# A four-layer graph kernel: layer 1 in another order, layer 2's walks in fp16 halves, layer 1's first halves made at the end of layer 0

## The reference

```
L0: H = adj != 0; h = relu(Dn * H @ (Be * H^T @ (x @ W1^T)) + b1); y = conv(layernorm(h), W2, b2)
L1: q, k, v = x @ W_qk, W_v; w = softmax over nodes(sum_m(q k^T / 8 * adj)); out = w * v
L2: T = rows normalised(adj * exp(leaky_relu(s_i + s_j))); H = sum_k (T^k x) @ Wk[k] + bk[k], k = 0, 1, 2; relu(H)
L3: A = rows normalised(exp(leaky(8 tanh((s_i + s_j) / 8))) * adj) * rowsum(adj); out = A @ x @ w
x = layernorm(x + L(x, adj))        after each of the four layers
```

## Time and profile before

| | |
|---|---|
| time, median of 3 runs | 778.45 us (775.82 to 780.42) |
| the profiled execution | 780.04 us |
| its span, first to last instruction | 778.1 us |
| busy: PE, DVE, ACT, POOL | 708.9, 548.5, 524.2, 320.9 us |
| mean granted clock of TensorE | 0.958 of full speed |

### The profile page before, as it was taken

One profiled execution on the slowest core, in us unless ns is written; L12 is line 12 of the kernel. 1 busy time (PEld: TensorE's weight loads), 2 busy tenths in 40 slices (PEclk: granted clock), 3 DMA queues, 4 the chain that ended last, 5 costly groups with the idle time before them and its releaser, 6 DMA issues.

```text
span 778.1 us, 18246 instructions
## 1 busy us (share of the span) xinstructions
PE 708.9 (91%) x5590; PEld 513.2 (66%) x5590; DVE 548.5 (70%) x1648; ACT 524.2 (67%) x1161; POOL 320.9 (41%) x402
## 2 busy tenths in 40 slices
PE   5899999999999983887787799999999997999995
PEld 5677777777777751554454566666666665878884
DVE  4888888888878742688878456666565654577995
ACT  4668887767777763566666555757575666688886
POOL 2243455434344434445454212323131313566773
PEclk9999999999999996999988699999999999899998
DMA  9422032232221003664435033231313121366663
GB/s 284 149 88 71 29 110 68 73 117 83 67 67 54 2 1 82 149 107 105 113 81 96 14 66 58 55 69 40 81 40 81 40 55 28 64 155 162 160 146 126
DMA packets 150733, 66.88 MB, mean 86 GB/s; under 512 B 104852, under 2 KB 148246, under 8 KB 150680
## 3 DMA queue, kind: packets, MB, share of 16 engines
q1 hardware_dynamic: 149088, 66.21, 34.7%
q10 hardware_dynamic: 1592, 0.01, 0.1%
HBM read 28.46 MB, written 8.39 MB: 47 GB/s over the span
## 4 chain that ended last, share of the span: by engine, by line
PE 45%; DVE 9%; issue 3%; DMA 2%; ACT 1%; POOL 1%; SPq 1%; DVEq 0%; ACTq 0%; POOLq 0%
PE bank L103 10%; PE bank L105 9%; PE bank L104 9%; PE bank L1449 4%; PE bank L1456 3%; PE bank L1721 3%; DVE l_st L1009 2%; DMA xT_lo<-x_lo_next 2%; PE bank L1372 2%; DVE l_pre L1252 2%; DVE l_mdiff L1016 1%; PE bank L1719 1%; PE bank L1177 1%; PE bank L1455 1%; PE bank L1463 1%
## 5 line engine op out<-in xcount | busy, mean ns | idle before, releaser
L1043 ACT ACTIVATE x_resident<-l_pre,l_nmr,l_rstd 128x256 f32 (+1 forms) x256 | 139.2, 600 | 39.4 <-POOL l_nmr L1037 39.3
L1094 POOL TENSOR_TENSOR x_lo_next<-x_resident,x_hi_next 128x1024 f16<-128x1024 f16 (+1 forms) x48 | 102.1, 2129 | 61.3 <-ACT x_hi_next L1087 60.2
L1009 DVE BATCH_NORM_STATS2 l_st<-l_pre 128x6 f32<-128x256 f32 x256 | 96.8, 415 | 1.1
L104 PE MATMUL bank<-Wk_hi,xT_lo 128*128 128x2 f16 (+2 forms) x384 | 95.4, 275 | 0.0
L103 PE MATMUL bank<-Wk_lo,xT_hi 128*128 128x2 f16 (+2 forms) x384 | 95.0, 276 | 0.4 <-ACT l_far L1508 0.4
L105 PE MATMUL bank<-Wk_hi,xT_hi 128*128 128x2 f16 (+2 forms) x384 | 94.1, 274 | 0.0
L1028 POOL TENSOR_TENSOR l_msum<-l_st 128x4 f32<-128x4 f32 x64 | 14.6, 228 | 180.3 <-DVE l_st L1009 180.3
L956 POOL TENSOR_TENSOR hq<-hq 128x512 f32<-128x512 f32 x32 | 43.1, 1347 | 77.2 <-ACT hq L701 77.2
L1034 POOL TENSOR_TENSOR l_rstd<-l_veps,minus_half 128x4 f32<-128x4 f32 x64 | 65.0, 1015 | 19.8 <-DVE l_veps L1023 17.5
L103 PE MATMUL bank<-W2T_lo,h_hi 128*128 128x257 f16 x256 | 70.1, 274 | 1.4 <-DVE h_lo L837 1.2
L105 PE MATMUL bank<-W2T_hi,h_hi 128*128 128x257 f16 x256 | 70.1, 274 | 0.0
(11 more groups left out here) (196 smaller groups left out, 2042.2 us busy)
## 6 DMA issues: line engine op xcount, KB each, us to landing
adj<-in_adj SPq DMA_DIRECT2D x32, 256.0 KB, 3.7
x_staged<-in_x SPq DMA_DIRECT2D x16, 512.0 KB, 3.7
x_resident<-in_x SPq DMA_DIRECT2D x16, 512.0 KB, 4.8
out<-x_resident SPq DMA_DIRECT2D x15, 512.0 KB, 3.2
l_adjT<-adjT_resident SPq DMA_DIRECT2D x16, 256.0 KB, 2.6
x_resident<-in_L_gnn_W SPq DMA_DIRECT2D x2, 512.0 KB, 5.5
x_resident<-in_L_gnn_Wk SPq DMA_DIRECT2D x1, 768.0 KB, 8.1
xT_hi<-x_hi_next SPq DMA_TRANSPOSE x48, 3.2
```

The source lines that it names most:

```text
L104: nc.tensor.matmul(out, lhs[1], rhs[0], start=False, stop=False, **kw)
L1009: dve.bn_stats(L.st[p][:, j, :], L.pre[p][:, j, :]).then_inc(L.st_ok, 1)
L1043: act.activation(K.x[:, gcols(g, j)], L.pre[p][:, j, :], ACT.Identity, bias=L.nmr[p][:, j:j + 1], scale=L.rstd[p][:, j:j + 1]).then_inc(L. ...
L1094: pool.tensor_tensor(F.xs[p][1][:], x_group(K, g), F.xs[p][0][:], ALU.subtract).then_inc(F.x_lo, 1)
```

## The change

1. `over_layers` puts the draining step of the old layer ahead of the new layer's step.
2. Layer 1's first two groups of x are split and transposed at the end of layer 0. The tiles for the halves of x and their transposes exist from the start; layer 0's staged x and its mixed x use the same memory.
3. Layer 1: residual and norm lag one step instead of two, each engine's order is new, small tiles and two PSUM banks are doubled. On ScalarE the high half of x stands ahead of the norms. One small operation of the softmax is folded into another.
4. Layer 2: T is split in halves on ScalarE and POOL and transposed by DMA; the far and middle results are split too, with the low halves on VectorE; each walk is a `triple` of fp16 products. The order of all engines is new, and the norm lags one step less.

The diff, cut to its core:

```diff
+            if 0 <= g + AFTER < drain:
+                before(G + g + AFTER, (g + AFTER) % 2, lambda k, g=g: g + AFTER + k < 0)
             if g >= -lead:
                 step(g, g % 2, lambda k, g=g: 0 <= g + k < G)
-            if 0 <= g + AFTER < drain:
-                before(G + g + AFTER, (g + AFTER) % 2, lambda k, g=g: g + AFTER + k < 0)
...
+        K.F = front(nc, ctx)
+        K.xst = [half[:].bitcast(F32).rearrange("p (g d) -> p g d", g=GP) for half in K.F.halves]
...
+        px = [[half[:].rearrange("p g d n -> p (g d n)").rearrange("p (d c) -> p d c", d=DT) for half in pair]
+              for pair in K.F.xT]
...
+                for g in range(2):
+                    for i in range(2):
+                        sp.wait_ge((K.F.x_hi, K.F.x_lo)[i], g + 1)
+                        sp.wait_ge(hid_ps, upto(G - 2 + g, HT, HT))
+                        sp.dma_start(K.F.xT[g][i][:].rearrange("p g d n -> p (g d) n"),
+                                     K.F.xs[g][i].rearrange("p g d -> p (g d)"),
+                                     transpose=True).then_inc(K.F.xT_in[g], 16)
...
+                def first_high(g):
+                    act.wait_ge(px_ps, upto(G - 2 + g, 2, 2))
+                    act.wait_ge(L.x_new, upto(g, GP, GP))
+                    act.activation(K.F.xs[g][0], x_group(K, g), ACT.Copy).then_inc(K.F.x_hi, 1)
...
+                    if isinstance(g, int) and g == G - 1:
+                        first_high(0)
+                        first_high(1)
...
+                def first_low(g):
+                    pool.wait_ge(K.F.x_hi, g + 1)
+                    pool.tensor_tensor(K.F.xs[g][1], x_group(K, g), K.F.xs[g][0], ALU.subtract).then_inc(K.F.x_lo, 1)
...
+                    if isinstance(g, int) and g == G - 2:
+                        first_low(0)
+                        first_low(1)
...
-    F.made = 2 if layer > 1 else 0
+    F.made = 2
...
             if has(-1):
-                score_rows(g - 1)
+                aggregate(g - 1, q)
+            if has(0):
+                project(g, p, 0)
+                project(g, p, 1)
+            if has(-1):
+                score_rows(g - 1, q)
             if has(0):
                 project(g, p, 2)
                 project(g, p, 3)
             if has(-1):
-                weight_columns(g - 1)
-            if has(0):
-                aggregate(g, p)
-            if has(1):
-                project(g + 1, q, 0)
-                project(g + 1, q, 1)
-        return step, 1, 1
+                weight_columns(g - 1, q)
+        return step, 0, 1
...
-            if has(-1):
-                exponentials(g - 1)
-            if has(0):
-                copy_qkv(g, p, 0)
-                copy_qkv(g, p, 1)
-                copy_qkv(g, p, 2)
-                copy_qkv(g, p, 3)
             if has(-2):
                 norm_apply(K, L, act, g - 2, p, 0)
                 norm_apply(K, L, act, g - 2, p, 1)
                 norm_apply(K, L, act, g - 2, p, 2)
                 norm_apply(K, L, act, g - 2, p, 3)
+            if has(0):
+                exponentials(g, p)
+            if has(1):
+                copy_qkv(g + 1, q, 0)
+                copy_qkv(g + 1, q, 1)
+                copy_qkv(g + 1, q, 2)
+                copy_qkv(g + 1, q, 3)
...
-            if has(-2):
-                residual(g - 2, p, 0)
-                residual(g - 2, p, 1)
-                norm_row(L, dve, g - 2, p, 0)
-                norm_row(L, dve, g - 2, p, 1)
             if has(-1):
-                scores(g - 1, q)
-            if has(-2):
-                residual(g - 2, p, 2)
-                residual(g - 2, p, 3)
-                norm_row(L, dve, g - 2, p, 2)
+                weights(g - 1, q)
+                residual(g - 1, q, 0)
+                residual(g - 1, q, 1)
+                residual(g - 1, q, 2)
+                residual(g - 1, q, 3)
+                norm_row(L, dve, g - 1, q, 0)
+                norm_row(L, dve, g - 1, q, 1)
+            if has(0):
+                scores(g, p)
             if has(-1):
-                maximum(g - 1)
-            if has(-2):
-                norm_row(L, dve, g - 2, p, 3)
-                norm_variance(L, dve, g - 2, p, EPS)
+                norm_row(L, dve, g - 1, q, 2)
+                norm_row(L, dve, g - 1, q, 3)
+            if has(0):
+                maximum(g, p)
             if has(-1):
-                softmax(g - 1)
-                weights(g - 1)
-        return step, 0, 2
+                norm_variance(L, dve, g - 1, q, EPS)
+            if has(0):
+                softmax(g, p)
+        return step, 0, 1
...
+        def transpose_T(g, p):
+            for s in range(2):
+                sp.wait_ge((t_hi, t_lo)[s], upto(g, 1, 1))
+                if s == 0 and reused(g):
+                    sp.wait_ge(out_ps, upto(g - 2, GP, GP))
+                sp.dma_start(tT[p][s][:], ts[s][:], transpose=True).then_inc(tT_in[p], 16)
+
         def step(g, p, has):
-            if has(2) and reused(g + 2):
-                sp.wait_ge(S.u_ok, upto(g, 1, 1))
-                load_adj(K, sp, g + 2, p)
+            if has(0):
+                transpose_T(g, p)
+            if has(2):
+                next_adj(g + 2, p)
             if halves_due(F, g + 2):
                 transpose_x(F, sp, g + 2, p, (near_ps, GP))
-        return step, 0, 0
+        return step, 2, 0
...
+        def walk_far(g, p, j):
+            turned(pe, g, p)
+            pe.wait_ge(far_hi, upto(g, GP, j + 1))
+            pe.wait_ge(far_lo, upto(g, GP, j + 1))
+            triple(nc, b_near[j][:, 0:D], [s[:, j, :] for s in tT[p]], [s[:] for s in far[j]],
+                   start=False, skip_group_check=True).then_inc(mid_ps, 1)
+
+        def walk_mid(g, p, j):
+            pe.wait_ge(mid_hi, upto(g, GP, j + 1))
+            pe.wait_ge(mid_lo, upto(g, GP, j + 1))
+            o = b_near[j][:, D:2 * D]
             pe.matmul(o, K.ones16[:], K.bkrow[:], start=False, stop=False, skip_group_check=True)
-            pe.matmul(o, tT[p][:, j * N:(j + 1) * N], mid[j][:], start=False, stop=True,
-                      skip_group_check=True).then_inc(out_ps, 1)
-
-        def transpose_T(g):
-            pe.wait_ge(tf_ok, upto(g, 1, 1))
-            pe.wait_ge(S.t_ok, upto(g, GP, GP))
-            for j in range(GP):
-                m = pe.transpose(b_t[:, j * N:(j + 1) * N], tf[:, j * N:(j + 1) * N], K.ident[:])
-            m.then_inc(tT_ps, 1)
+            triple(nc, o, [s[:, j, :] for s in tT[p]], [s[:] for s in mid[j]],
+                   start=False, skip_group_check=True).then_inc(out_ps, 1)
...
-            if has(-1):
-                walk_far(g - 1, q, 0, 0)
-                project_far(g - 1, q, 2)
-                walk_far(g - 1, q, 1, 1)
-                walk_mid(g - 1, q, 0, 0)
-                project_far(g - 1, q, 3)
-                project_near(g - 1, q, 2, 2)
-                walk_far(g - 1, q, 2, 2)
-                project_near(g - 1, q, 3, 0)
-                walk_far(g - 1, q, 3, 0)
-                walk_mid(g - 1, q, 1, 1)
-                walk_mid(g - 1, q, 2, 2)
-                walk_mid(g - 1, q, 3, 0)
-            if has(0):
-                project_far(g, p, 0)
-                project_near(g, p, 0, 0)
-                transpose_T(g)
-                project_far(g, p, 1)
+                walk_mid(g - 1, q, 3)
             if has(1):
                 node_scores(nc, K, F, S, pe, g + 1, q, b_s, K.wk, D)
+            if has(0):
+                project_near(g, p, 0)
+                project_near(g, p, 1)
+            if has(1):
+                spread_scores(nc, K, S, pe, g + 1, b_t, S.t_ok, GP)
+            if has(0):
+                project_far(g, p, 2)
+                project_far(g, p, 3)
+                project_near(g, p, 2)
+                project_near(g, p, 3)
+                walk_far(g, p, 0)
+                walk_far(g, p, 1)
+                walk_far(g, p, 2)
+                walk_far(g, p, 3)
+                walk_mid(g, p, 0)
+            if has(1):
+                project_far(g + 1, q, 0)
+            if has(0):
+                walk_mid(g, p, 1)
+                walk_mid(g, p, 2)
+            if has(1):
+                project_far(g + 1, q, 1)
...
+        def T_high(g, p):
+            act.wait_ge(tf_ok, upto(g, 1, 1))
+            if reused(g, 1):
+                turned(act, g - 1, 1 - p)
+            act.activation(ts[0][:], tf[:], ACT.Copy).then_inc(t_hi, 1)
...
+        def far_low(g, j):
+            dve.wait_ge(far_hi, upto(g, GP, j + 1))
+            if reused(g, 1):
+                dve.wait_ge(mid_ps, upto(g - 1, GP, j + 1))
+            dve.tensor_tensor(far[j][1][:], b_far[j % 2][:, 0:D], far[j][0][:], ALU.subtract).then_inc(far_lo, 1)
...
+        def mid_low(g, j):
+            dve.wait_ge(mid_hi, upto(g, GP, j + 1))
+            if reused(g, 1):
+                dve.wait_ge(out_ps, upto(g - 1, GP, j + 1))
```

(41 more changed lines are left out.)

257 lines of the change are left out of this document (115 added, 142 removed).

## The result

The changed kernel took 785.2 us (median of 20), the kernel before 780.2 us (median of 20, 775.8 to 783.7): a ratio of 1.0049, with a 95% interval of 1.0029 to 1.0070. The ratio leaves out two executions of the changed kernel that fell in a slower state (790.4 and 832.6); the others lie between 777.6 and 789.1. The forecast was 751.

The account below looks back on a forecast made before the run. Layer 1 was taken as set by VectorE, layer 2 by TensorE time. Terms of -5.1 - 8.5 - 1 - 13 = -27.6 us on 778.4 gave 751, with 736 to 775 for 8 in 10.

Parts of the forecast that it names:

- Part 1: Passage from layer 0 to 1: first halves and transposes of x leave the chain, -5.1 us after costs.
- Part 2: Layer 1's new order: step from 7.38 to 6.8 us, -8.5 us over 15 steps, between -19 and +12.
- a collision in one step of three: Layer 1: POOL's low half starts before VectorE's fourth residual in a third of steps, adding 0.7 us to 6.1.
- the forecast's own sign for it: Sign of a wrong forecast: layer 1 residuals of over 2 us, ending with POOL's low half.
- without collision: Layer 1 step if POOL's low half holds up no VectorE operation: 7.38 - 1.1 - 0.15 = 6.1 us.
- rival B: Layer 1: POOL's low half collides with VectorE's fourth residual in every step, 21 us more, 772; chance 0.16.
- A saving that was right in size: Layer 1: the difference of the means no longer meets POOL's low half, 1.28 - 0.17 = 1.1 us off each step.
- a lower clock in layer 2: Sign of a wrong forecast: lower granted clock in layer 2 because TensorE now waits in each step; no size given.
- Part 3: Passage from layer 1 to layer 2: second spread at about +14 us, -1 us, bounds -2 and +3.
- Part 4: Layer 2's fp16 walks and DMA transposes of T: step from 13.35 to 12.5 us, -13, bounds -19 and 0.
- loop through the transposes of x: Layer 2: node scores to last near projection, then DMA transposes of x, close in 12.5 us, over TensorE's 12.1.
- Rival E: Slower, 786, chance 0.08: layer 1 collides every step (8.2, +21); layer 2's T low half meets a residual (13.4, +14).

Follow-up runs that it names:

- the three versions that keep the order: Changed kernel with POOL's low half in layer 1 cut to 32 features (748.3 us) or 128 (760.0), or with extra TensorE products filling its wait (775.6).
- With the clock held up: Changed kernel with twelve more fp16 products per step of layer 1, run while TensorE waits, results unread: 775.6 us, ratio 0.9942 to the kernel before.
- the base version: Changed kernel with ScalarE's high half of x in layer 1 behind the first norm operation only: 751.1 us, ratio 0.9625 to the kernel before.
- taking away their wait: The base version with layer 2's node scores of the next group behind TensorE's first near projection: 743.6 us, ratio 0.9547 to the kernel before.
- when the step was 12.38: The base version with layer 2's exponentials of the next group ahead of ScalarE's norm operations: 749.9 us, ratio 0.9614 to the kernel before.

## Why the prediction was wrong

- **Part 1, right at its place.** -5.1 forecast, -4.7 measured; what is left of it at the end is open (nothing to 6 us).
- **Part 2, the step that failed: "I take a collision in one step of three: 6.1 + 0.7 = 6.8".** The collision is in every step, and the step takes 8.55 us on average, not 6.8; the forecast's own sign for it, residuals of over 2 us that end with POOL's low half, is what the trace shows (2.40). Its pieces were right: without collision 6.1 forecast, 6.16 measured; the full price is POOL's operation; POOL at +3.1 from the start of the exponentials forecast, +2.96 measured (330.90 - 327.94); the fourth residual at +3.05 to +3.1 forecast, +2.97 measured (330.91 - 327.94), so the tie was even nearer than the forecast had it. But the order of the two does not vary from step to step. POOL's start moves from 2.95 us behind the exponentials' to 4.72 where the clock is low, the residuals move with it, and a residual is held in 15 steps of 15, and in the 45 steps of the three versions that keep the order as well. The text had this argument, under rival B, and gave B 0.16. Its case of one step in three occurs in none of these versions. (The sum has a slip besides: (6.8 - 7.38) x 15 is -8.7.)
- **A saving that was right in size, by luck in part.** The forecast took 1.1 us off every step, from one step in which the difference took 1.28 us. Over the layer that operation took 0.16 to 1.33 us, 0.75 on average, and in five steps VectorE waited for TensorE ahead of the maximum, 5.4 us in all. The step without a collision came out at 6.16 because both went, and the forecast counted only the first.
- **A term that was missing, the clock.** Rival B's bound for all steps was 8.2 us, and at full clock it holds (7.97). The half clock adds 8.7 us to the layer. The text named a lower clock in layer 2 as something to look for. In layer 1 it took stretches at half clock only as something that shifts the tie, and put no price on more of them; there TensorE's busy share fell from 89.1 / 110.1 = 81% to 94.5 / 128.2 = 74%.
- With +18.2 in place of -8.5, the forecast's own sum gives 751 + 26.7 = 778, which is near the profiled execution (777.9). The median is 7 us above that, and why a typical execution is slower than the profiled one stays open: there is no trace of one, and the mean granted clocks on record don't tell (0.949 at the median against 0.954, but 0.948 for the fastest of all, 777.6 us, and 0.955 for one of 787.0). With the clock held up, nine executions lay between 771 and 777.
- **Part 3**: -1 forecast, -2.2 measured, a little past its bound of -2.
- **Part 4, right in size, and in the ordinary step for another reason.** 12.5 us forecast, 12.54 measured; -13 forecast, -9.9 and -3.3 measured, 15.0 by the run that puts the old layer back. TensorE's own work was forecast well: 12.1 us, and in five ordinary steps of the base version (505.46 to 568.15) it is busy 60.50 us, 12.1 a step. But the 0.44 us on top are no loop through the transposes of x. In these steps TensorE waits 2.2 us, all of it for the halves of mid (lines above), at the end of a loop that the forecast did not have: logits, leaky, exponentials behind three norms, transition, halves of mid. The transposes bind where they land late, and hardly elsewhere: taking away their wait saved 6 us in three early steps and left the ordinary one at 12.54. That they stand just behind mid is suggested by one wait of 0.2 us in five steps when the step was 12.38, and not shown beyond that. So the number 12.5 came out right by luck in part.
- **Rival E** came nearest in time (786), and only its half in layer 1 is true. In the changed kernel's layer 2 the transition product takes 0.69 us in every step, where it took 1.53, and T's low half meets a residual once (0.71 us in place of 0.42); the low half of x holds one leaky relu at the layer's start (1.86 us in place of 0.69).
